# Two transformer layers on one core: weights of two key quarters added on GpSimd, and the query rests of a pair formed in one instruction

## The chip, the cores and the metric

The kernel runs on one core of one Trainium2 chip. The metric is the time of one execution on the device, in microseconds (us). The engines of the core are TensorE (PE in the profile, its weight loads PEld), VectorE (DVE), ScalarE (ACT), GpSimd (POOL) and SyncE (SP, whose queue issues DMAs). They run side by side and meet at semaphores.

## The reference, cut to what matters

Eight rows (sequences) of 512 tokens with 128 channels go through two layers. Each layer adds attention and a feed-forward part to its input. The change touches the attention of layer 1, with 16 query heads of 64 channels that share one set of keys and values:

```python
q = (x @ Wq + bq).reshape(B, S, H, DK)        # H = 16, DK = 64
k = x @ Wk + bk
v = x @ Wv + bv
scores = jnp.einsum('bshd,btd->bhst', q, k) / np.sqrt(DK)
w = jax.nn.softmax(scores, axis=-1)
out = jnp.einsum('bhst,btd->bshd', w, v).reshape(B, S, H * DV)
return out @ Wo + bo
```

The feed-forward part of layer 1 picks two of eight experts for each token. Layer 0 has an attention without softmax and a feed-forward part with weights and inputs rounded to four bits.

## The kernel before, in words

Every engine runs the same list of steps. A row of layer-1 attention is a round of 64 steps (k = 0 to 63), eight rounds in all (r = 0 to 7). A step handles one quarter of the keys (128) against all 512 queries of one head: `first` (L1446) computes the transposed scores in two matmuls (L1459, L1460), ScalarE exponentiates them into one of six buffers `wide` (L856). Two heads form a pair, eight steps of k: even steps one head, odd steps the other. Every fourth step, two steps later, `values` (L1470) takes four finished tiles: for each it runs two matmuls of 32 columns with the values (L1487), into bank `ps_out[0]`, and then one with a tile of ones (L1498), into `ps_out[1]`, which sums the weights over the keys, that is, gives the softmax's denominator. The four positions of 32 columns in the array hold the two heads and two key quarters side by side. The operands are float32, and each such matmul is two records in the profile. For the last two pairs of the last round (`direct`) the ones have their own form (L1495), left aside here.

At the end of a pair ScalarE copies both banks (L882, L887). SyncE stores the two partial sums per head, reloads them turned, VectorE adds and inverts them (L1227, L1228), and SyncE spreads the inverses (`sums_and_inverses`, L516). VectorE multiplies (L1241).

The scores use a split of the query into a rounded part and a rest. For each pair `query` makes 128 channels (two heads) in one bank of a ring of four (`ps_small`), ScalarE rounds it into `q_x` (L786), SyncE copies its halves four times into `q_hh` (L550), and VectorE's `lo_q` (L1031) writes the two rests straight into `q_lm`, one instruction per head (L1039). The maxima over keys come from matmuls (L1413) that go through the same ring, and VectorE reduces each (L1047).

In between lie the pieces of layer 0 for the next row (`l0`), placed at steps by `L0_AT` and, for VectorE, by `L0_DVE`, the gates and slots of the experts, and the projection (L1519). A layer norm needs an inverse root that GpSimd makes (`root`, L645). GpSimd further subtracts for the split of the expert weights in round 0 (L705), clears (L676) and scatters (L690) the experts' input rows, and scatters their results (L718). Its program before is a plain sequence: all that of one kind, then the next, each waiting for its data.

In round 7 the 23 expert tiles are inserted as steps of their own after k = 15, 23 and 31.

## Time and profile before

| | us |
|---|---|
| median of 3 runs | 1330.49 |
| lowest, highest | 1329.61, 1333.75 |
| the profiled execution, its own time | 1337.21 |
| its span in the trace | 1335.5 |
| mean granted clock of TensorE | 0.971 of full speed |

Busy time is the union of an engine's instructions; the chain is the work that ended last, followed back from the end. A matmul's end is modelled, so the pace of TensorE is read from the starts of neighbouring records. In the rows below a line number is that of the kernel before.

### The profile page before, as it was taken

What the parts mean: (1) busy time and instruction counts of PE and PEld (TensorE: products, weight loads), DVE (VectorE), ACT (ScalarE), POOL (GpSimd) and SP (SyncE); (2) the same over time, 40 slices, a digit from 0 to 9 for tenths busy, and PEclk for the clock granted to TensorE, in tenths of its full rate; (3) what the DMA queues carried; (4) which work ended last, traced back from release to release, by engine and by line L of the source; (5) the groups of instructions that cost most, each with busy time, mean ns of one, the idle gap of its engine ahead of it and who ended that gap; (6) DMA issues with size and microseconds to landing.
All of it is one profiled execution on the core that took longest, in us unless ns stands there. A gap on an engine that the chain in (4) does not pass through costs nothing.

```text
span 1335.5 us, 21832 instructions
## 1 busy us (share of the span) xinstructions
PE 1231.2 (92%) x7185; PEld 723.1 (54%) x7185; DVE 1008.1 (75%) x2396; ACT 682.9 (51%) x1252; POOL 262.2 (20%) x311
## 2 busy tenths in 40 slices
PE   5469999999999999999999999999999989999987
PEld 3235445554555455555554555455545468676743
DVE  6876888578867885788578857885787667677765
ACT  4036555544554456445544554455444466776631
POOL 2023223100210012001200120012000227263620
PEclk9559999999999999999999999999999989999988
DMA  2063574212321232224122412241221456474451
GB/s 79 0 174 100 187 211 153 62 50 58 115 64 49 58 113 58 58 57 113 49 62 54 120 42 61 63 119 36 61 67 46 155 164 233 139 241 159 132 199 48
DMA packets 89779, 133.80 MB, mean 100 GB/s; under 512 B 33292, under 2 KB 49228, under 8 KB 85700
## 3 DMA queue, kind: packets, MB, share of 16 engines
q1 hardware_dynamic: 75108, 99.80, 26.3%
q0 software_dynamic: 11344, 31.64, 7.2%
q8 instruction: 59, 0.97, 0.3%
q10 hardware_dynamic: 3216, 0.97, 0.3%
q14 instruction: 52, 0.43, 0.1%
HBM read 59.86 MB, written 38.68 MB: 74 GB/s over the span
## 4 chain that ended last, share of the span: by engine, by line
PE 63%; DVE 23%; issue 4%; ACT 3%; SPq 2%; DMA 2%; POOL 1%; another core or an unknown queue 0%; ACTq 0%; DVEq 0%; POOLq 0%
PE bank L1487 13%; PE bank L1459 6%; PE bank L1498 6%; PE bank L1413 5%; DVE mneg L1047 5%; PE bank L1460 5%; PE bank L1315 4%; PE bank L1317 4%; PE bank L1316 4%; DVE q_lm L1039 3%; PE bank L1519 3%; PE bank L1331 2%; PE bank L1321 2%; PE bank L1366 2%; PE bank L1356 1%
## 5 line engine op out<-in xcount | busy, mean ns | idle before, releaser
L856 ACT ACTIVATE wide<-bank 128x512 f32<-128x512 f32 x512 | 295.8, 600 | 324.1 <-PE bank L1460 314.2
L1047 DVE TENSOR_REDUCE mneg<-bank 128x1 f32<-128x512 f32 x512 | 329.4, 685 | 136.9 <-PE bank L1413 131.3
L1487 PE MATMUL bank<-wide,v_w 128*32 128x512 f32 x2048 | 248.0, 602 | 1.3 <-issue 1.0
L1459 PE MATMUL bank<-q_hh,k_hl 128*128 128x512 f32 x512 | 233.2, 456 | 14.3 <-ACT wide L856 11.1
L1460 PE MATMUL bank<-q_lm,k_h 65*128 65x512 f32 x512 | 203.6, 398 | 0.0
L1459 PEld LDWEIGHTS bank<-q_hh,k_hl 128*128 128x128 f32 x512 | 96.6, 189 | 135.6 <-issue 80.5
L649 POOL TENSOR_TENSOR rs<-rs,power 128x4 f32<-128x4 f32 x24 | 24.5, 1021 | 631.4 <-DVE rs L930 631.3
L1498 PE MATMUL bank<-wide,ones 128*32 128x512 f32 x992 | 129.2, 592 | 0.0
L718 POOL DMA_INDIRECT y_rows<-y_m,to_u x92 | 101.7, 1106 | 125.3 <-DVE y_m L1173 103.1
L1487 PEld LDWEIGHTS bank<-wide,v_w 128*32 128x32 f32 x2048 | 53.7, 109 | 122.7 <-issue 114.7
L1413 PE MATMUL bank<-k_a,q_x 128*128 128x512 f32 x256 | 107.5, 420 | 8.0 <-ACT hqt L776 2.6
L1039 DVE SCALAR_TENSOR_TENSOR q_lm<-bank,bq,q_x 64x512 fp32r<-64x512 f32 x128 | 95.6, 747 | 13.9 <-issue 11.5
L1413 PE MATMUL bank<-k_b,q_x 128*128 128x512 f32 x256 | 103.5, 404 | 2.3 <-DVE mneg L1047 2.1
L1460 PEld LDWEIGHTS bank<-q_lm,k_h 65*128 65x128 f32 x512 | 97.5, 190 | 11.6 <-issue 1.4
L690 POOL DMA_INDIRECT x_rows<-xr,slot_u x64 | 63.8, 997 | 170.3 <-DVE slot_u L1119 135.1
L882 ACT ACTIVATE raw<-bank 128x512 f32<-128x512 f32 x64 | 38.3, 598 | 107.9 <-PE bank L1498 93.4
L1281 DVE TENSOR_TENSOR part_l<-wide,part_h 128x512 fp32r<-128x512 f32 x92 | 62.0, 691 | 37.0 <-ACT wide L861 33.7
L861 ACT ACTIVATE part_h<-bank,b_t 128x512 fp32r<-128x512 f32 x92 | 63.5, 691 | 31.5 <-PE bank L1317 24.0
L1498 PEld LDWEIGHTS bank<-wide,ones 128*32 128x32 f32 x992 | 32.4, 111 | 74.9 <-issue 74.9
L1519 PE MATMUL bank<-wo,on 128*128 128x128 f32 x512 | 61.8, 280 | 4.8 <-DVE on L1241 4.8
L1413 PEld LDWEIGHTS bank<-k_a,q_x 128*128 128x128 f32 x256 | 49.1, 192 | 31.8 <-ACT q_x L786 13.5
L1519 PEld LDWEIGHTS bank<-wo,on 128*128 128x128 f32 x512 | 61.2, 196 | 7.4 <-DVE on L1241 6.2
(252 smaller groups left out, 1955.7 us busy)
## 6 DMA issues: line engine op xcount, KB each, us to landing
q_hh<-q_x SPq DMA_DIRECT2D x256, 128.0 KB
w_t<-w_rows SPq DMA_DIRECT2D x23, 1024.0 KB
x_rows<-part_h POOLq DMA_DIRECT2D x65, 258.0 KB, 5.0
inv<-inverse_scratch SPq DMA_DIRECT2D x124, 128.0 KB, 2.9
w_rows<-w_t SPq DMA_DIRECT2D x8, 1024.0 KB, 5.0
x_m<-x_rows SPq DMA_DIRECT2D x23, 258.0 KB
stage<-in_L_ffn_W SPq DMA_DIRECT2D x16, 256.0 KB, 4.7
yab<-y_rows POOLq DMA_DIRECT2D x8, 512.0 KB, 8.4
```

The source lines that it names most:

```text
L690: pool.indirect_dma_start(x_rows, bass.IndirectOffsetOnAxis(ap=slot_u[:, b, i:i + 1], axis=0), xr[:, i, :], None).then_inc(scattered, 16)
L718: pool.indirect_dma_start(y_rows, bass.IndirectOffsetOnAxis(ap=to_u[:, t % TO, i:i + 1], axis=0), y_m[:, t % YM, i, :], None).then_inc(y_s ...
L856: act.activation(wide[:, st.g % WIDE, :], ps, ACT.Exp, scale=SCALE1).then_inc(wide_full, 1)
L861: ins = act.activation(dst, ps, ACT.Gelu_apprx_tanh, bias=b_t[:, st.t % WT, st.m:st.m + 1])
L1039: ins = dve.scalar_tensor_tensor(q_lm[0:DK, gh % HEADS, :], ps[rows, :], bq[rows, h:h + 1], q_x[rows, pair % 2, :].bitcast(F32), ALU.add, ...
L1047: dve.tensor_reduce(mneg[:, pair % 2, col:col + 1], ps[:], X, ALU.max, negate=True).then_inc(free, 1)
L1413: into(("mx", 2 * pair + b, j), lambda ps: pe.matmul(ps[:], q_x[:, pair % 2, P * j:P * j + P], keys[:, n % 2, :], start=True, stop=True))
L1459: pe.matmul(ps, k_hl[:, n, t], q_hh[:, gh % HEADS, :], start=True, stop=False)
L1460: last = pe.matmul(ps, k_h1[0:DK + 1, n, t], q_lm[0:DK + 1, gh % HEADS, :], start=False, stop=True)
L1487: pe.matmul(ps_out[0][rows, :], v_w[:, n, c, TILE * d:TILE * d + TILE], weights, start=(c == 0), stop=(c == TT - 1))
L1498: last = pe.matmul(ps_out[1][rows, :], ones[:], weights, start=(half == 0), stop=(half == 1))
L1519: last = pe.matmul(ps[:, P * i:P * i + P], on[:, g % (H // 4), P * i:P * i + P], wo[:, g, :], start=(g == pairs.start), stop=(g == pairs.s ...
```

## The change

For each pair but the two direct ones, GpSimd adds the exponentiated tiles of two key quarters of the same head (steps k and k - 2, where k modulo 4 is 2 or 3), in two pieces of 256 columns, into `halves`. `values` no longer has the ones. `sums_of` runs four matmuls with ones once per pair, three steps after the pair's last, on the four added tiles; the two positions per head now hold the two half sums. ScalarE's copy of the sums comes one step later and waits for them (`summed`); ScalarE's reuse of a `wide` buffer waits for the addition too, and an addition waits for the previous pair's `summed`. VectorE's `lo_q` becomes one instruction for 128 channels into a single buffer `q_rest`, and SyncE copies its halves to `q_lm` (`copy_rests`); the semaphore for the copies of a pair counts to 96 instead of 64. GpSimd's program becomes one list over the steps, with roots, additions, splits, scatters and clearings at given steps. Besides, memory is laid over: `part_l` over weights of layer 0, `stage` over two of the four expert weight buffers, so that round 0 splits weights in two buffers instead of four.

```diff
-    L0_DVE = [-14, -11, -11, -10, -7, -6, -4, -2, 0, 0, 9, 10, 13, 17, 18, 21, 25, 26, 29, 30, 30, 31, 32,
-              34, 35, 37, 38, 39, 40, 42, 43, 44, 44]
+    L0_DVE = [-14, -13, -11, -10, -7, -6, -4, -2, 0, 0, 9, 10, 13, 17, 18, 21, 25, 26, 29, 30, 30, 32, 32,
+              34, 35, 37, 38, 39, 40, 42, 42, 44, 44]
...
+    ROOT_AT = [31, 43, 52]
+    SCATTER_AT = [[1, 4, 5, 8], [13, 16, 17, 20]]
+    LAST_SCATTER_AT = [[0, 0, 0, 0], [1, 1, 1, 1]]
+    ZERO_AT = [24, 25, 28, 29, 32, 33, 36, 37]
...
+    def adds(st):
+
+        return st.kind == "o" and st.k % TT >= 2 and added(pair_of(st))
...
-            names = [(("pv", pair), 0), (("ps", pair), 1)]
+            names = [(("pv", pair), 0)] + ([(("ps", pair), 1)] if direct(pair) else [])
+        elif st.kind == "o" and st.k % PAIR == PAIR - 1 and added(pair_of(st)):
+            names = [(("ps", pair_of(st)), 1)]
...
-        q_x = sb("q_x", [P, 2, S], F32R)
+        q_x, q_rest = sb("q_x", [P, 2, S], F32R), sb("q_rest", [P, S], F32R)
+        halves = sb("halves", [P, 2, 2, S])
...
+            def copy_rests(pair):
+
+                read_out(sp, ("q", pair))
+                for b in range(2):
+                    gh, here = 2 * pair + b, slice(DK * b, DK * b + DK)
+                    if gh >= HEADS:
+                        sp.wait_ge(first_full, last_step(gh - HEADS) + 1)
+                    sp.dma_start(q_lm[0:DK, gh % HEADS, :].bitcast(F32), q_rest[here, :].bitcast(F32)).then_inc(q_copied[pair % 2], 16)
...
+                if split_pair(st) is not None:
+                    copy_rests(split_pair(st))
...
+            def halve(st):
+
+                half, b, pair = st.k % PAIR // TT, st.k % 2, pair_of(st)
+                if pair:
+                    pool.wait_ge(summed, pair)
+                pool.wait_ge(wide_full, st.g + 1)
+                for q in range(2):
+                    cols = slice(S // 2 * q, S // 2 * q + S // 2)
+                    last = pool.tensor_tensor(halves[:, half, b, cols], wide[:, (st.g - 2) % WIDE, cols],
+                                              wide[:, st.g % WIDE, cols], ALU.add)
+                last.then_inc(halved, 1)
...
-            scatter(0)
-            for j in range(2 * E):
-                if SPLIT_STEPS[j] in (27, 45):
-                    root()
-                e, second = divmod(j, 2)
-                pool.wait_ge(expert_h, j + 1)
-                hi, lo = (w_t[:, e % WT, 2 * second + d, :] for d in range(2))
-                pool.tensor_tensor(lo, stage[:, j % 4, :], hi.bitcast(F32), ALU.subtract).then_inc(expert_l, 1)
-            for n in range(1, NB):
-                if n > 1:
-                    root()
-                    root()
-                if n + 1 < NB:
-                    root()
-                    zero(n + 1)
-                scatter(n)
-            for t in range(TILES):
-                read_out(pool, ("ty", t))
-                pool.wait_ge(to_set, t + 1)
-                for i in range(TT):
-                    pool.indirect_dma_start(y_rows, bass.IndirectOffsetOnAxis(ap=to_u[:, t % TO, i:i + 1], axis=0),
-                                            y_m[:, t % YM, i, :], None).then_inc(y_scattered[t % TO], 16)
+
+            for st in steps:
+                if st.kind == "o":
+                    if st.k in (ROOT_AT if st.r < NB - 2 else ROOT_AT[0:2] if st.r == NB - 2 else ()):
+                        root()
+                    if adds(st):
+                        halve(st)
+                    if st.r == 0 and st.k in SPLIT_STEPS:
+                        split_rest(SPLIT_STEPS.index(st.k))
+                    for b, at_ in enumerate(SCATTER_AT if st.r < NB - 1 else LAST_SCATTER_AT):
+                        for i in range(TT):
+                            if st.k == at_[i]:
+                                scatter(st.r, b, i)
+                    if st.k in ZERO_AT and st.r + 2 < NB:
+                        zero(st.r + 2, ZERO_AT.index(st.k))
+                if st.g is not None:
+                    here, i = divmod(st.g - 3, TT)
+                    if here - 2 in tile_of:
+                        scatter_y(tile_of[here - 2], i)
...
+                        if st.g - WIDE in add_of:
+                            act.wait_ge(halved, add_of[st.g - WIDE])
...
-                pair = pair_end(st, 1)
+                pair = pair_end(st, 2)
                 if pair is not None and not direct(pair):
-                    act.wait_ge(second_done, last_step(2 * pair + 1) + 1)
+                    act.wait_ge(summed, pair + 1)
...
-                for b in range(2):
-                    gh, rows = 2 * pair + b, slice(DK * b, DK * b + DK)
-                    h = gh % H
-                    if gh >= HEADS:
-                        dve.wait_ge(first_full, last_step(gh - HEADS) + 1)
-                    ins = dve.scalar_tensor_tensor(q_lm[0:DK, gh % HEADS, :], ps[rows, :], bq[rows, h:h + 1],
-                                                   q_x[rows, pair % 2, :].bitcast(F32), ALU.add, ALU.subtract)
-                ins.then_inc(free, 1)
+                if pair:
+                    dve.wait_ge(q_copied[(pair - 1) % 2], ((pair - 1) // 2 + 1) * 96)
+                p = pair % (H // 2)
+                dve.scalar_tensor_tensor(q_rest[:], ps[:], bq_two[:, p:p + 1], q_x[:, pair % 2, :].bitcast(F32),
+                                         ALU.add, ALU.subtract).then_inc(free, 1)
...
+            def sums_of(pair):
+
+                free_bank(("ps", pair))
+                pe.wait_ge(halved, add_of[last_step(2 * pair + 1)])
+                for half in range(2):
+                    for b in range(2):
+                        rows = slice(DK * b + TILE * half, DK * b + TILE * half + TILE)
+                        last = pe.matmul(ps_out[1][rows, :], ones[:], halves[:, half, b, :], start=True, stop=True)
+                last.then_inc(summed, 1)
...
-                            pe.matmul(ps_out[0][rows, :], v_w[:, n, c, TILE * d:TILE * d + TILE], weights,
-                                      start=(c == 0), stop=(c == TT - 1))
+                            last = pe.matmul(ps_out[0][rows, :], v_w[:, n, c, TILE * d:TILE * d + TILE], weights,
+                                             start=(c == 0), stop=(c == TT - 1))
+                        if added(pair):
+                            last.then_inc(second_done, 1)
+                if added(pair):
+                    return
                 for c in range(2 * half, 2 * half + 2):
                     for b in range(2):
                         weights = wide[:, (st.g - 3 + 2 * (c % 2) + b) % WIDE, :]
-                        if direct(pair):
-                            for d in range(2):
-                                rows = slice(DK * b + TILE * d, DK * b + TILE * d + TILE)
-                                last = pe.matmul(ps_out[1][rows, :], ones[:], weights, start=(c == 0), stop=(c == TT - 1))
-                        else:
-                            rows = slice(DK * b + TILE * (c % 2), DK * b + TILE * (c % 2) + TILE)
-                            last = pe.matmul(ps_out[1][rows, :], ones[:], weights, start=(half == 0), stop=(half == 1))
+                        for d in range(2):
+                            rows = slice(DK * b + TILE * d, DK * b + TILE * d + TILE)
+                            last = pe.matmul(ps_out[1][rows, :], ones[:], weights, start=(c == 0), stop=(c == TT - 1))
                         last.then_inc(second_done, 1)
...
+                pair = pair_end(st, 1)
+                if pair is not None and added(pair):
+                    sums_of(pair)
```

## Rows read from the trace of the kernel before

**Rows 1.** Page part 1: busy us, share of the span, instructions of each engine

```profile
PE 1231.2 (92%) x7185; PEld 723.1 (54%) x7185; DVE 1008.1 (75%) x2396; ACT 682.9 (51%) x1252; POOL 262.2 (20%) x311
```

**Rows 2.** Page part 4: the chain that ended last, by engine and by line

```profile
PE 63%; DVE 23%; issue 4%; ACT 3%; SPq 2%; DMA 2%; POOL 1%; another core or an unknown queue 0%; ACTq 0%; DVEq 0%; POOLq 0%
PE bank L1487 13%; PE bank L1459 6%; PE bank L1498 6%; PE bank L1413 5%; DVE mneg L1047 5%; PE bank L1460 5%; PE bank L1315 4%; PE bank L1317 4%; PE bank L1316 4%; DVE q_lm L1039 3%; PE bank L1519 3%; PE bank L1331 2%; PE bank L1321 2%; PE bank L1366 2%; PE bank L1356 1%
```

**Rows 3.** Windows: busy of PE, PEld, DVE, ACT, POOL, then clock, DMA

```profile
351.00:432.00 81.00, 79.48 (x483) 43.90 (x482) 58.48 (x130) 43.48 (x80) 8.04 (x9) 1.00 0.24 64
432.00:486.04 54.04, 51.51 (x323) 29.51 (x319) 45.96 (x129) 25.00 (x49) 7.62 (x12) 1.00 0.28 80
```

**Rows 4.** Chain by line of 351 to 432 us, then 432 to 486.04

```profile
by line: PE bank L1487 20.6%; PE bank L1459 10.3%; PE bank L1498 9.5%; PE bank L1413 8.1%; PE bank L1460 8.1%; PE bank L1519 4.4%; PE bank L1366 3.2%; issue 3.1%; PE bank L1356 3.0%; PE bank L1348 2.7%; PE bank L1331 2.4%; PE bank L1335 2.4
...
by line: DVE mneg L1047 15.1%; PE bank L1487 10.3%; DVE q_lm L1039 8.0%; PE bank L1498 5.6%; PE bank L1413 5.3%; PE bank L1459 4.2%; issue 4.0%; POOL rs L649 3.8%; PE bank L1460 3.5%; PE bank L1377 3.2%; PE bank L1315 2.4%; PE bank L1317 2.
```

**Rows 5.** Page part 5: name, count, busy us, mean ns, idle before

```profile
L1039 DVE SCALAR_TENSOR_TENSOR q_lm<-bank,bq,q_x 64x512 fp32r<-64x512 f32 x128 | 95.6, 747 | 13.9 <-issue 11.5
...
L1498 PE MATMUL bank<-wide,ones 128*32 128x512 f32 x992 | 129.2, 592 | 0.0
```

**Rows 6.** Timeline of PE: start us, us, engine, line, operation, count

```profile
566.40 1.04 PE L1498 MATMUL bank<-wide,ones 128*32 128x512 f32 x8
567.37 0.51 PE L1459 MATMUL bank<-q_hh,k_hl 128*128 128x512 f32 x1
567.71 0.40 PE L1460 MATMUL bank<-q_lm,k_h 65*128 65x512 f32 x1
567.95 0.40 PE L1413 MATMUL bank<-k_a,q_x 128*128 128x512 f32 x1
...
570.08 0.40 PE L1460 MATMUL bank<-q_lm,k_h 65*128 65x512 f32 x1
570.41 0.64 PE L1487 MATMUL bank<-wide,v_w 128*32 128x512 f32 x4
```

**Rows 7.** Groups by form on VectorE, one round, 351 to 486.04 us

```profile
L1056 DVE TENSOR_TENSOR x_l<-bank,x_h 128x512 fp32r<-128x512 f32 x1 | 0.7, 684 | 0.0
```

**Rows 8.** L662 and L705 on GpSimd: count, duration in ns min/median/max

```profile
L662 POOL TENSOR_TENSOR wk_l<-raw,wk_h x2: 311/325/339, 27.8 to 28.1; 128x64 fp32r<-128x64 f32 x2
...
L705 POOL TENSOR_TENSOR w_t<-stage,w_t x16: 1269/1282/1614, 119.2 to 205.7; 128x512 fp32r<-128x512 f32 x16
```

**Rows 9.** Four lines of VectorE: count, duration in ns min/median/max

```profile
L902 DVE TENSOR_SCALAR qs<-qs x43: 178/178/718, 9.1 to 981.2; 128x22 f32<-128x22 f32 x33, 128x32 f32<-128x32 f32 x8, 128x24 f32<-128x24 f32 x2
...
L910 DVE TENSOR_SCALAR t<-t x43: 343/344/1310, 10.4 to 985.2; 128x352 uint32<-128x352 uint32 x33, 128x512 uint32<-128x512 uint32 x8, 128x384 uint32<-128x384 uint32 x2
...
L934 DVE SCALAR_TENSOR_TENSOR rs<-rs x24: 161/163/1246, 6.9 to 1001.8; 128x4 f32<-128x4 f32 x24
...
L935 DVE TENSOR_TENSOR rs<-rs x24: 161/163/1207, 7.1 to 1002.0; 128x4 f32<-128x4 f32 x24
```

**Rows 10.** Timeline, subtractions of GpSimd beside one instruction of VectorE

```profile
163.00 2.51 POOL L705 TENSOR_TENSOR w_t<-stage,w_t 128x512 fp32r<-128x512 f32 x2
163.04 1.25 DVE L934 SCALAR_TENSOR_TENSOR rs<-rs 128x4 f32<-128x4 f32 x1
```

**Rows 11.** Timeline of SyncE's queue, four copies of queries

```profile
1047.25 3.19 SPq L550 DMA_DIRECT2D q_hh<-q_x  x4
```

**Rows 12.** Timeline of GpSimd, eight scatters before the last round

```profile
1037.13 1.04 POOL L690 DMA_INDIRECT x_rows<-xr,slot_u  x1 [35.27 <-DVE slot_u L1119]
...
1047.59 0.96 POOL L690 DMA_INDIRECT x_rows<-xr,slot_u  x1 [0.30 <-issue]
```

**Rows 13.** Timeline of ACT: exponentials of k 63 and 0, then of k 6

```profile
1038.57 1.09 ACT L856 ACTIVATE wide<-bank 128x512 f32<-128x512 f32 x2 [0.33 <-PE bank L1460]
...
1051.44 0.60 ACT L856 ACTIVATE wide<-bank 128x512 f32<-128x512 f32 x1 [2.74 <-PE bank L1460]
```

More of the change, by code:

```diff
@@ L188, in direct, with added, pair_of @@
         return pair >= (NB - 1) * (H // 2) + DIRECT
+    def added(pair):
+        return not direct(pair)
+    def pair_of(st):
+        return st.r * (H // 2) + st.k // PAIR
+    def adds(st):
+        return st.kind == "o" and st.k % TT >= 2 and added(pair_of(st))
     def tile_end(st):
@@ L408, in two_layers @@
         expert_h, expert_l = sem("expert_h"), sem("expert_l")
-        w_stored = [sem(f"w_stored{i}") for i in range(4)]
+        w_stored = [sem(f"w_stored{i}") for i in range(2)]
         small_full = [sem(f"small_full{i}") for i in range(SMALL)]
@@ new lines, in _ @@
+            for n in range(2):
+                for e in range(E):
+                    zero(n, e)
+            root()
+            for st in steps:
+                if st.kind == "o":
+                    if st.k in (ROOT_AT if st.r < NB - 2 else ROOT_AT[0:2] if st.r == NB - 2 else ()):
+                        root()
+                    if adds(st):
+                        halve(st)
[11 more added lines that the diff above has]
+                        scatter_y(tile_of[here - 2], i)
@@ L1474, in values @@
                 if half == 0:
-                    for name in (("pv", pair), ("ps", pair)):
-                        b, uses = out_place[name]
-                        if uses:
-                            pe.wait_ge(out_free[b], uses)
+                    free_bank(("pv", pair))
+                    if direct(pair):
+                        free_bank(("ps", pair))
                     if st.k == TT - 1:
```

87 lines of the change are left out of this document (54 added, 33 removed).

## Prediction

> **What bounds the kernel now.** I read the sums of the page first [rows 1]. TensorE shows 92% busy, VectorE 75%, GpSimd 20%, so TensorE is the first suspect and GpSimd has room. Busy is not the path, so the chain that ended last comes next [rows 2]: 63% of it is TensorE, 23% VectorE, 3% ScalarE, 1% GpSimd. The matmuls of the ones (L1498), which the change halves, are 6% of the chain, some 80 us of 1335.5, and the query rests (L1039), also halved, 3%, some 40 us. Then the windows: one round of attention, 351 to 486 us, has two parts [rows 3]. For 81 us TensorE is 79.5 us busy and VectorE only 58.5. For the last 54 us VectorE has 46.0 us of work (layer norms, gates, slots, next to the same maxima), and the chain there runs through VectorE's maxima at 15.1% and the rests at 8.0% [rows 4]. In the first part L1498 is 9.5% of the chain, in the second 5.6% [rows 4]: 7.7 and 3.0 us. So seven rounds are led first by TensorE and then by VectorE and TensorE in turn. The last round is filled up with the expert tiles, which the change leaves as they are.
>
> **Part 1, half of the tiles of ones go.** L1498 has 992 records [rows 5], 16 per pair, so 62 pairs. One block of eight starts at 566.40 and what follows it at 567.37: 0.97 us of TensorE, two blocks a pair [rows 6]. After the change each pair has one block: 62 x 0.97 = 60 us less. But the block no longer stands behind the products of values; it stands alone among score matmuls. Behind such an f32 block the next start-to-start step is 0.34 us (567.37 to 567.71) where the one after it is 0.24; ahead of one it is 0.33 (570.08 to 570.41) [rows 6]. So an isolated block costs another 0.10 + 0.09 us, about 0.19: 62 x 0.19 = 12 us back, and 48 us of TensorE's time stay. The chain has 10.7 us of L1498 in a round that spends 8 x 2 x 0.97 = 15.5 us on it, a share of 0.69 (over the kernel: 80 us of 120, 0.67). 48 x 0.67 = 32 us. Bounds: 12 us, if only the last part of the round counted and VectorE ate the rest, and 48. I take 32, as the two views agree.
>
> **Part 2, the query rests in one instruction.** Two instructions of 64x512 at 747 ns each [rows 5] become one of 128x512. The trace has no such form on 128 partitions; the nearest row, a VectorE subtraction of 128x512 with one operand in PSUM, takes 684 ns [rows 7]. The duration goes by columns, so the new one is put at 0.75 us, between 0.68 and 0.76. 64 pairs lose one of 747 ns: 48 us of VectorE. The chain has 40 us of the 95.6 [rows 2, 5], half goes: 20 us. Bounds: 10 us, if TensorE is late next in half of the places, and 25. The halves then travel by two more copies per pair on SyncE's queue. Four copies of the same kind take 3.19 us there [rows 11], 0.8 each, so 1.6 us per pair of 17 us (135 us by 8). They are wanted 13 steps later, at the pair's first scores, so I cost them at nothing; the cover is those 13 steps, and without it each pair would wait for a transfer of some us. The queue now waits at step 3 of eight for VectorE's rest, with the store of the sums behind it, and behind that the inverses. Those are used over ten steps later.
>
> **Part 3, the additions on GpSimd.** 62 pairs x 4 = 248 additions of 128x512 in two pieces each. GpSimd's nearest rows: 1282 ns for a two-input 128x512, 325 ns for 64 columns [rows 8]. A line through both gives 0.73 us for 256 columns; half of 1282 is 0.64. So an addition is 1.3 to 1.5 us, and a pair asks 5.1 to 5.8 us of GpSimd in 17. It has the room: it was busy 15.7 us in this round [rows 3]. A pair's last addition is ready some 2 us after its exponential, and TensorE asks for it three steps later, with a block of values in between. So in general it is hidden. ScalarE's reuse of a buffer of the ring of six asks for it four steps later.
>
> What isn't hidden is what it does to VectorE. In round 0 GpSimd already runs 16 such subtractions, and beside them VectorE's small instructions stretch: L902 718 ns against a median of 178, L910 1310 against 344, L934 1246 against 163, L935 1207 against 163 [rows 9]. L934 started at 163.04, just behind GpSimd's 163.00, and ended as the first of its two ended [rows 10]. The four are 0.54 + 0.97 + 1.08 + 1.04 = 3.63 us, by 16 additions 0.23 us each. 248 x 0.23 = 57 us more for VectorE, more than part 2 gives it. Of that about 0.3 lies on the path: VectorE is 23% of the whole chain [rows 2], and more where its small instructions are dense. 0.3 x 57 = 17 us. Bounds: 0, if the collisions fall in VectorE's idle time, and 57.
>
> The Trainium skill ("SBUF — State Buffer", section "Who interferes with whom") speaks against this change here: a VectorE instruction with two SBUF inputs, or in a 2-port mode, and a GpSimd instruction that reads SBUF exclude each other, and the second one waits for the whole of the first. The stretched rows agree, and by the rule a reader of PSUM such as the maxima stays free. By it two pieces give VectorE two waits of up to 0.64 us where one piece gave one of up to 1.28. A sum by the rule would put the same 57 us of delay at nearly the same size, so it stands.
>
> **Part 4, order on GpSimd.** The program's order is now one list by steps. A root (L649) can stand behind an addition, and VectorE's norm waits for it; GpSimd's roots are 3.8% of the chain in the second part [rows 4]. At three roots a round and 0.1 us more each: 2 us in all, between 0 and 8. In the last round eight scatters stand at steps 0 and 1, ahead of the additions of steps 2 and 3. They took 1037.13 to 1048.55, 11.4 us [rows 12]. Now they begin behind the addition of step 63, whose exponential ended at 1039.1 [rows 13], so at about 1041, and end at 1052.4. The addition of step 2 ends at 1053.8, and the exponential of step 6, at 1051.44 before [rows 13] and a us earlier now, waits for it: 3 to 4 us, once. I take 4, between 0 and 7.
>
> **Part 5, costed at nothing.** Buffers moved over one another, two weight buffers in round 0 instead of four (a store is asked for seven steps, some 15 us, ahead of its reuse), the few shifted steps of VectorE's list, and ScalarE's copy of the sums one step later.
>
> **The sum** is made against the profiled execution, 1337.21 us with a span of 1335.5: -32 - 20 + 17 + 2 + 4 = -29. The runs' median is 1330.49, 0.5% lower, and takes the same -29: 1301.5 us, a ratio of 0.978.
>
> **Rivals.** (a) The gain arrives nearly whole: collisions fall into VectorE's idle time, 22% of a round. For it: VectorE has 22 us idle in the first part [rows 3]. Against it: its dense work lies in the second part. -32 - 20 + 2 = -50, so 1280. (b) The path passes to the coupling of VectorE and TensorE and most of the gain is off the path: 12 of part 1, 10 of part 2, 17 and some 3 back, about -2 to -6, so 1326. For it: VectorE is 85% busy in the second part already; against it: the first part, 60% of the round, is TensorE's. (c) Slower: the two pieces of an addition each cost VectorE as much as one whole did, since tiny instructions in sequence are caught once per piece, as L934 and L935 were [rows 9]. Then an addition costs 0.46 us, 114 us in all, and two thirds of it reach the end, as maxima queue behind them and TensorE waits for their banks: +76 - 52 + 2 + 4 = +30, so 1360. It decides from 0.19 us per addition that reaches the end (46 of gain over 248). My forecast has 0.07. (d) The additions come late and TensorE waits for `halved` each pair, 0.5 us or more: -29 + 31 = +2, so 1333. For it: GpSimd is shared with roots that wait for VectorE; against it: the margin above.
>
> **How the numbers follow.** About 0.3%, 4 us, is what a measurement of this kernel can tell from no change. The forecast, with its own range of 1285 to 1318, has a chance of 0.58, (a) 0.18, (b) 0.10, (c) 0.09, (d) 0.05. Faster: 0.58 + 0.18 + 0.06 of (b) = 0.82. Same: 0.04 + 0.02 of (d) = 0.06. Slower: 0.09 + 0.03 = 0.12. The range reaches over (a) and (b), with the wider bounds of parts 1 to 3: 1273 to 1328.
>
> **What would show it.** The line of ones has half its records and its blocks stand alone; round time falls from 135 us to 131 or so, mostly in the first part. The rests show 64 instructions near 0.75 us. VectorE's two-input and SBUF-only instructions show raised means while the maxima stay at 685 ns. GpSimd's additions take 0.6 to 0.75 us a piece. TensorE's waits name GpSimd in no more than a few places, the last round's start among them. The prediction is wrong if VectorE's busy time rises by over 60 us with TensorE waiting for maxima, or if waits for GpSimd stand ahead of the ones in every pair.

## The result and the profile after

The changed kernel takes 1362.78 us, the median of four runs (1358.39 to 1369.60). The kernel before takes 1330.05 us beside it, in four runs (1328.62 to 1333.75). The ratio is 1.0245, with a 95% interval of 1.0209 to 1.0282: slower by some 33 us, where 29 us of gain were forecast. The time lies outside the range of 1273 to 1328. The profiled execution took 1363.96 us with a span of 1362.2.

The page of the changed kernel, part 1 and one line of part 2 (the granted TensorE clock in 40 slices, in tenths):

```profile
PE 1218.4 (89%) x6689; PEld 712.9 (52%) x6689; DVE 1022.2 (75%) x2332; ACT 681.9 (50%) x1252; POOL 638.0 (47%) x807
...
PEclk9569888999999999999998999999999989998988
```

Against [rows 1], TensorE ran 496 matmuls less and was busy only 12.8 us less, where 48 were forecast. VectorE lost 64 instructions of 747 ns, 48 us, and was busy 14.1 us more. The mean granted clock fell from 0.971 to 0.944.

Its groups, from part 5 of the page (busy us, mean ns of one | idle before, and what ended it):

```profile
L745 POOL TENSOR_TENSOR halves<-wide 128x256 f32<-128x256 f32 x496 | 379.6, 790 | 483.0 <-PE bank L1544 296.3
...
L1109 DVE TENSOR_REDUCE mneg<-bank 128x1 f32<-128x512 f32 x512 | 328.6, 683 | 130.5 <-PE bank L1475 127.0
...
L1544 PE MATMUL bank<-halves,ones 128*32 128x512 f32 x496 | 66.9, 612 | 0.3 <-POOL halves L745 0.2
```

The groups by form on VectorE, in the changed kernel:

```profile
L1303 DVE TENSOR_TENSOR on<-raw,inv 128x512 f32<-128x512 f32 x62 | 54.4, 877 | 10.9 <-DMA inv<-inverse_scratch 10.7
...
L1102 DVE SCALAR_TENSOR_TENSOR q_rest<-bank,bq_two,q_x 128x512 fp32r<-128x512 f32 x64 | 47.8, 747 | 9.2 <-issue 7.9 <-PE bank L1379 0.8
...
L1058 DVE TENSOR_TENSOR v<-v,lnw_row 128x512 f32<-128x512 f32 x8 | 9.2, 1149 | 0.0
```

and the first and the last of these in the kernel before:

```profile
L1241 DVE TENSOR_TENSOR on<-raw,inv 128x512 f32<-128x512 f32 x62 | 42.6, 686 | 8.8 <-DMA inv<-inverse_scratch 8.5
...
L993 DVE TENSOR_TENSOR v<-v,lnw_row 128x512 f32<-128x512 f32 x8 | 5.5, 686 | 0.0
```

The ones have half their records, and TensorE never stands ahead of them for GpSimd: 0.3 us of idle time in all. The rests are one instruction on 128 partitions, in the 747 ns that half of one took [rows 5]. The maxima, which read PSUM, keep their length (683 ns). What has grown most is VectorE's work with two operands in SBUF: the normalization of outputs takes 877 ns instead of 686, the layer norm's weights 1149 instead of 686. Some instructions with a single SBUF tensor have grown too. The one below took 348 ns before and 388 with the fills of experiment 2. Three such lines (L979, L1004, L1156) are 11 us longer in all than with the fills.

```profile
L979 DVE TENSOR_SCALAR t<-t 128x352 f32<-128x352 f32 x33 | 18.0, 545 | 0.2
```

One place in the middle of a round shows it (start, us, engine; in brackets the idle time before):

```profile
462.08 4.00 POOL L745 TENSOR_TENSOR halves<-wide 128x256 f32<-128x256 f32 x4 [1.10 <-ACT wide L921]
462.46 1.22 DVE L1058 TENSOR_TENSOR v<-v,lnw_row 128x512 f32<-128x512 f32 x1
...
463.71 1.11 DVE L1059 TENSOR_TENSOR v<-v,lnb_row 128x512 f32<-128x512 f32 x1
...
464.85 1.29 DVE L1109 TENSOR_REDUCE mneg<-bank 128x1 f32<-128x512 f32 x2
...
465.69 0.47 PE L1475 MATMUL bank<-k_a,q_x 128*128 128x512 f32 x1 [1.60 <-DVE mneg L1109]
```

Two layer-norm instructions are stretched beside four pieces of additions. The two maxima behind them start late, and TensorE stands still for 1.60 us until they have freed a bank. This is the step from a collision to the end of the kernel. The direct way, TensorE or ScalarE waiting for an addition, is nearly empty over the whole run. It is 0.2 us for TensorE, and this for ScalarE (who waits for whom: us in all, times, longest):

```profile
ACT wide L921 <- POOL halves L745: 2.1, 2, 1.4
```

**Where the time went.** I cut the span at the starts of ScalarE's copy of the bank of values, one per pair, 64 in all: to the first one, then eight pairs (round 0), 48 (rounds 1 to 6), and the end. The windows of after (us, busy of PE, PEld, DVE, ACT and POOL with instructions, granted clock, DMA share, GB/s):

```profile
0.00:119.91 119.91, 74.15 (x288) 47.02 (x289) 86.80 (x254) 43.24 (x85) 31.19 (x61) 0.77 0.35 90
119.91:271.76 151.85, 133.82 (x706) 71.95 (x707) 115.01 (x244) 76.26 (x144) 84.05 (x100) 0.91 0.51 151
271.76:1079.40 807.64, 756.11 (x4359) 417.39 (x4360) 631.15 (x1471) 396.54 (x755) 387.07 (x506) 0.98 0.33 85
1079.40:1362.20 282.80, 254.31 (x1339) 176.49 (x1339) 189.26 (x364) 165.82 (x269) 135.70 (x140) 0.94 0.53 169
```

and of the three attention windows of before, which no row ahead of the prediction cuts in this way:

```profile
123.72:258.95 135.23, 128.22 (x770) 69.58 (x770) 106.58 (x253) 75.30 (x144) 35.74 (x36) 1.00 0.51 154
258.95:1057.63 798.68, 773.28 (x4743) 431.01 (x4743) 619.14 (x1517) 398.66 (x755) 89.08 (x117) 1.00 0.26 71
1057.63:1335.50 277.87, 254.44 (x1371) 176.06 (x1370) 192.08 (x369) 165.66 (x269) 107.81 (x100) 0.96 0.51 166
```

The span grew by 26.7 us (the profiled execution of before was itself 6.7 us above its median): -3.8 ahead of the first mark, +16.6 in round 0, +9.0 in rounds 1 to 6, +4.9 at the end. Within a round (marks of a middle round; column i is the time from pair i's mark to the next, and so holds the steps of pair i + 1; worked out, not a view):

```
i                          0     1     2     3     4     5     6     7
before                  13.8  17.4  12.9  16.7  16.2  19.2  23.1  15.8
after                   12.7  16.9  12.3  18-20 16.8  20.3  21.9  16.3
change with fills       13.1  16.9  13.1  15.1  14.6  16.8  21.9  16.3
```

In columns 0, 1, 2 and 6 the change brings 0.5 to 1.2 us, where part 1 forecast 0.78 of TensorE per pair; in 7 it loses 0.5. In 3 to 5, where VectorE leads, it loses up to 3 us. The last line is an experiment below.

### The profile page after: what moved, and what is told of

The parts are those of the page before. It is cut to its first block and busy times, and to the rows that moved or that the text cites. A ratio compares the mean times of both kernels' runs of the same rounds, so it can differ in the third digit from the quotient of the medians.

```text
span 1362.2 us, 21768 instructions
## 1 busy us (share of the span) xinstructions
PE 1218.4 (89%) x6689; PEld 712.9 (52%) x6689; DVE 1022.2 (75%) x2332; ACT 681.9 (50%) x1252; POOL 638.0 (47%) x807
## 5 line engine op out<-in xcount | busy, mean ns | idle before, releaser
L745 POOL TENSOR_TENSOR halves<-wide 128x256 f32<-128x256 f32 x496 | 379.6, 790 | 483.0 <-PE bank L1544 296.3
L1563 PE MATMUL bank<-wide,v_w 128*32 128x512 f32 x2048 | 260.8, 629 | 1.0 <-issue 1.0
L1521 PE MATMUL bank<-q_hh,k_hl 128*128 128x512 f32 x512 | 237.9, 465 | 18.4 <-ACT wide L921 10.9
L1544 PE MATMUL bank<-halves,ones 128*32 128x512 f32 x496 | 66.9, 612 | 0.3 <-POOL halves L745 0.2
L1475 PEld LDWEIGHTS bank<-k_b,q_x 128*128 128x128 f32 x256 | 50.2, 196 | 25.7 <-DVE mneg L1109 14.2
L926 ACT ACTIVATE wide<-bank,b_t 128x512 f32<-128x512 f32 x92 | 62.9, 684 | 0.0
```

The lines of the kernel that those rows point to most:

```text
L745: last = pool.tensor_tensor(halves[:, half, b, cols], wide[:, (st.g - 2) % WIDE, cols], wide[:, st.g % WIDE, cols], ALU.add)
L926: ins = act.activation(dst, ps, ACT.Gelu_apprx_tanh, bias=b_t[:, st.t % WT, st.m:st.m + 1])
L1475: into(("mx", 2 * pair + b, j), lambda ps: pe.matmul(ps[:], q_x[:, pair % 2, P * j:P * j + P], keys[:, n % 2, :], start=True, stop=True))
L1521: pe.matmul(ps, k_hl[:, n, t], q_hh[:, gh % HEADS, :], start=True, stop=False)
L1544: last = pe.matmul(ps_out[1][rows, :], ones[:], halves[:, half, b, :], start=True, stop=True)
L1563: last = pe.matmul(ps_out[0][rows, :], v_w[:, n, c, TILE * d:TILE * d + TILE], weights, start=(c == 0), stop=(c == TT - 1))
```

## The experiments

Times compare with before on the same chip, as a ratio with its interval. Where I turn a ratio into microseconds, it is times 1330. Each theory's expectation was written before the run.

**1. Part 2 alone, and the change without part 2.**

```diff
 # e1: before, with this; likewise copy_rests on SyncE, counts 96
-                for b in range(2):
-                    ins = dve.scalar_tensor_tensor(q_lm[0:DK, gh % HEADS, :], ps[rows, :], bq[rows, h:h + 1], ...
+                dve.scalar_tensor_tensor(q_rest[:], ps[:], bq_two[:, p:p + 1], q_x[:, pair % 2, :].bitcast(F32),
+                                         ALU.add, ALU.subtract).then_inc(free, 1)
 # e2: the change, with the same lines the other way round
```

> The kernel before with only the rests of a pair formed in one instruction and copied by SyncE (and small buffers of the expert table laid over the comparisons, to make room). Theory (GpSimd's additions are what costs): this part is worth what it was put at, 10 to 25 us, so 1305 to 1320. Rival (the two more copies per pair hold SyncE's queue or come late): 1330 or more, with TensorE or SyncE waiting for copies of q_lm.

> The changed kernel with the rests formed as before, one instruction per head straight into q_lm. Theory: the rests bring 10 to 25 us in the changed kernel too, so this one takes 1373 to 1388. Rival (the rests by copy cost): 1350 or less.

The rests alone: 1326.48 us, ratio 0.9984 (0.9966 to 1.0001), so 2 us, hardly told from nothing. The change without them: 1382.04 us, ratio 1.0379 (1.0316 to 1.0443), so 50 us slower. So the additions and their list are the loss, and part 2 is worth 18 us on top of them (50 - 33, uncertain by some 10) but 2 by itself. VectorE's busy time fell as forecast, by 51 us (956.7 against 1008.1):

```profile
PE 1222.6 (93%) x7185; PEld 722.6 (55%) x7185; DVE 956.7 (72%) x2332; ACT 680.9 (52%) x1252; POOL 258.7 (20%) x311
```

Its profiled execution had a span of 1320.0, 15.5 less than before's. But that was the lowest of ten runs of this kernel, and before's profiled one was 6.7 us above its median. So I take the ratio, not the two spans.

**2. The same change without GpSimd's reads.** In this kernel GpSimd fills the buffer of halves with ones instead of adding weights; the sums over the keys are left out.

```diff
-                    last = pool.tensor_tensor(halves[:, half, b, cols], wide[:, (st.g - 2) % WIDE, cols],
-                                              wide[:, st.g % WIDE, cols], ALU.add)
+                    last = pool.memset(halves[:, half, b, S // 2 * q:S // 2 * q + S // 2], 1.0)
```

> The changed kernel with each addition replaced by two fills of the same pieces with ones: the sums over keys are wrong, all waits stay, GpSimd writes only and each piece takes some 0.3 us instead of 0.79. Theory (reads of GpSimd's additions hold up VectorE): VectorE's on (L1303) goes back from 877 to 685 ns, its busy time falls by about 60 us, the clock rises, and the time is 1285 to 1310. Rival (the order of GpSimd's list and its waits for summed cost): 1340 or more, and VectorE's durations matter little.

1306.88 us, ratio 0.9828 (0.979 to 0.9866): 23 us faster than before, 55 us faster than the change by the two ratios. Its page, its groups and rounds 1 to 6:

```profile
PE 1191.9 (92%) x6689; PEld 703.9 (54%) x6689; DVE 956.3 (74%) x2332; ACT 681.9 (53%) x1252; POOL 398.9 (31%) x807
```

```profile
L744 POOL MEMSET halves<- 128x256 f32 x496 | 141.9, 317 | 625.9 <-PE bank L1542 314.3 <-ACT wide L919 310.6 <-issue 0.9
...
L1301 DVE TENSOR_TENSOR on<-raw,inv 128x512 f32<-128x512 f32 x62 | 42.4, 684 | 10.7 <-DMA inv<-inverse_scratch 6.1 <-issue 4.4
```

```profile
259.90:1015.98 756.08, 737.52 (x4359) 414.27 (x4360) 580.30 (x1471) 396.96 (x755) 201.56 (x506) 1.00 0.34 91
```

Every instruction count is that of the change. VectorE is busy 956.3 us instead of 1022.2, and the normalization is back at 684 ns. TensorE, with the same 6689 matmuls, is busy 1191.9 instead of 1218.4: 26.5 us of its busy time in the change are the same work done more slowly, at a mean granted clock of 0.944 over the run where this kernel has 0.964. Of these, 18.6 us lie in rounds 1 to 6 (756.11 to 737.52) and 7.7 in round 0 (133.82 to 126.12). The profiled execution here was the lowest of its four runs (1299.45), which the comparisons of single executions below flatter by up to 7 us. But a fill differs from an addition in two ways, its reads and its length (317 against 790 ns). Experiments 5 and 6 take these up.

**3. The change's list without any additions.** All 62 pairs keep their 16 tiles of ones.

```diff
-        return not direct(pair)
+        return not direct(pair) and False
 # and in values(): the plain pairs' ones as before
```

> The changed kernel with no pair added: ones run as in the kernel before, GpSimd has no additions but works by the list over the steps, the rests are formed in one instruction, buffers are laid over as in the change. Theory: the list alone costs under 5 us against the rests alone, 1305 to 1325. Rival (the list's order, and two weight buffers in round 0, are the cause): over 1335, with round 0 longer than before by over 10 us.

1326.94 us, ratio 0.9962 (0.9943 to 0.9982). So halving the ones is worth 1.3% of ratio, 18 us (0.9962 to 0.9828), and the additions' reads and length cost 4.2%, 55 us (0.9828 to 1.0245). From the intervals, each of these two differences is uncertain by some 6 to 7 us. The windows of this kernel, round 0 and rounds 1 to 6:

```profile
120.82:265.05 144.23, 132.37 (x770) 71.31 (x770) 99.31 (x245) 75.20 (x144) 40.84 (x45) 0.96 0.56 168
265.05:1044.67 779.62, 767.29 (x4743) 431.48 (x4743) 579.38 (x1469) 396.83 (x755) 86.34 (x113) 1.00 0.34 87
```

In rounds 1 to 6 TensorE's busy time falls from 767.29 here to 737.52 with the ones halved: 29.8 us for 48 pairs, 0.62 each, where 0.97 - 0.19 = 0.78 was forecast. And round 0 takes 144.2 us, against 135.2 before and 136.8 with the rests alone: the list itself costs there.

**4. One piece instead of two.**

```diff
-                for q in range(2):
-                    cols = slice(S // 2 * q, S // 2 * q + S // 2)
-                    last = pool.tensor_tensor(halves[:, half, b, cols], wide[:, (st.g - 2) % WIDE, cols], ...
+                last = pool.tensor_tensor(halves[:, half, b, :], wide[:, (st.g - 2) % WIDE, :],
+                                          wide[:, st.g % WIDE, :], ALU.add)
```

> The changed kernel with each addition as one instruction of 512 columns instead of two of 256. Theory (what counts is how long GpSimd reads): VectorE's delay per addition stays, 1355 to 1372. Rival (c) of the prediction (each piece catches an instruction of its own): half of the delay goes, some 30 us, so 1340 or less.

1377.62 us, ratio 1.0367 (1.0321 to 1.0412): 16 us slower than the change. Its groups:

```profile
L743 POOL TENSOR_TENSOR halves<-wide 128x512 f32<-128x512 f32 x248 | 325.6, 1318 | 543.9 <-PE bank L1542 323.4 <-ACT wide L919 218.4 <-issue 0.3
...
L1301 DVE TENSOR_TENSOR on<-raw,inv 128x512 f32<-128x512 f32 x62 | 62.3, 1006 | 10.6 <-DMA inv<-inverse_scratch 10.5
```

One piece holds GpSimd for less in all (325.6 against 379.6 us), yet VectorE is busy 1036.8 us instead of 1022.2. So two pieces are the better form, and rival (c), by which it was the pieces that double the cost, is wrong in its mechanism.

**5. A GpSimd instruction that reads one operand.** The copy takes the place of the addition, so one key quarter of each two is left out of the sums.

```diff
-                    last = pool.tensor_tensor(halves[:, half, b, cols], wide[:, (st.g - 2) % WIDE, cols],
-                                              wide[:, st.g % WIDE, cols], ALU.add)
+                    last = pool.tensor_copy(halves[:, half, b, cols], wide[:, st.g % WIDE, cols])
```

> The changed kernel with each addition replaced by a copy of one of its two operands, in the same two pieces: the sums miss half of the keys, all waits stay, GpSimd reads one operand instead of two. Theory (GpSimd's reads hold VectorE for as long as they last): pieces of 0.3 to 0.4 us, VectorE's on (L1303) at 700 to 780 ns, and a time between that of the fills (1307) and of the change (1363): 1310 to 1335. Rival (only two-operand additions do it): 1307 or less and on at 685 ns.

1307.14 us, ratio 0.9843 (0.981 to 0.9875), not to be told from the fills.

```profile
L745 POOL COPY halves<-wide 128x256 f32<-128x256 f32 x496 | 202.6, 438 | 573.1 <-PE bank L1543 294.3 <-ACT wide L920 278.3
...
L1302 DVE TENSOR_TENSOR on<-raw,inv 128x512 f32<-128x512 f32 x62 | 44.0, 709 | 10.1 <-DMA inv<-inverse_scratch 9.9
```

VectorE is busy 962.3 us, 6 more than with fills, where the additions make it 66 more. By length alone 438/790 of 66 would be 37 us. Yet a copy does hold VectorE. In each kernel some normalizations start together with a piece on GpSimd (start, us; with additions of 256 columns, of 512, with copies, with fills; x2 is two pieces):

```profile
449.13 1.27 DVE L1303 TENSOR_TENSOR on<-raw,inv 128x512 f32<-128x512 f32 x1
449.13 1.86 POOL L745 TENSOR_TENSOR halves<-wide 128x256 f32<-128x256 f32 x2
...
868.69 1.82 DVE L1301 TENSOR_TENSOR on<-raw,inv 128x512 f32<-128x512 f32 x1
868.69 1.27 POOL L743 TENSOR_TENSOR halves<-wide 128x512 f32<-128x512 f32 x1
...
816.83 0.94 DVE L1302 TENSOR_TENSOR on<-raw,inv 128x512 f32<-128x512 f32 x1
816.84 1.20 POOL L745 COPY halves<-wide 128x256 f32<-128x256 f32 x2
...
938.68 0.68 DVE L1301 TENSOR_TENSOR on<-raw,inv 128x512 f32<-128x512 f32 x1
938.68 0.55 POOL L744 MEMSET halves<- 128x256 f32 x2
```

By itself the normalization takes 0.68 us. Beside an addition whose first piece took 0.72 it takes 0.59 longer, beside one of 1.27 it takes 1.14 longer, beside a copy of 0.39 it takes 0.26 longer, and beside a fill of 0.30 no longer. So where both start together, VectorE is held for the length of GpSimd's instruction less 0.13 us, whether that reads one operand or two, and this instruction isn't held at all where GpSimd only writes. What parts copies from additions is first of all their length: a meeting costs 0.26 us instead of 0.59. If meetings also become fewer by the same factor, 66 us shrink to 13 (an estimate from these numbers). Why only 6 arrive, that is, which instructions the shorter pieces happen to meet, was not followed up.

The Trainium skill ("SBUF — State Buffer", section "Who interferes with whom") says that a VectorE instruction with two SBUF inputs contends with a GpSimd instruction that reads SBUF. The trace agrees: additions (686 to 877 ns on average) and copies (709 ns on average, 0.94 us at the meeting above) hold such an instruction, fills don't (684), and the maxima, which read PSUM, don't move beside additions (683).

**6. VectorE's delay without any collision.** Is it VectorE's lost time that reaches the end, or something else that additions do? This kernel is the one with fills, and VectorE runs 33 small extra instructions in each of rounds 1 to 6, in steps 34 to 57, where the collisions were densest.

```diff
+                    if 0 < st.r < NB - 1:
+                        for _ in range(extra.get(st.k, 0)):
+                            link(dve.tensor_tensor(pad[:], pad[:], pad[:], ALU.add))
 # pad is 128x48; extra gives 1 or 2 in 22 of the steps 34 to 57
```

> The run with fills in place of additions (1307 us, sums wrong), plus 33 small VectorE instructions of some 0.22 us on a scratch tile in steps 34 to 57 of rounds 1 to 6, that is the 7 us a round by which VectorE's busy time grew there through the additions, with nothing on GpSimd. Theory (the whole loss is VectorE's time in the part where TensorE waits for its maxima, and the clock that falls with each wait): rounds 1 to 6 grow from 127.7 us to 133 to 138, as in the change (136.5), with a clock under 1.00 in pairs there, and the whole to 1335 to 1365. Rival (GpSimd's late additions hold up TensorE or ScalarE, beyond VectorE's time): rounds stay under 131 us and the whole under 1325.

1341.38 us beside 1340.07 for before, ratio 1.0018 (0.9991 to 1.0045): 25 us more than the fills alone (0.9828). The added group and rounds 1 to 6:

```profile
L1339 DVE TENSOR_TENSOR pad<-pad 128x48 f32<-128x48 f32 x198 | 40.4, 204 | 4.5
```

```profile
260.70:1052.33 791.63, 747.57 (x4359) 415.29 (x4360) 617.67 (x1669) 397.63 (x755) 199.02 (x506) 0.99 0.33 87
```

Over rounds 1 to 6, against the fills' window: VectorE busy +37.4 us, the stretch +35.6. The change against the fills: VectorE busy +50.9, the stretch +51.6. In both, by profiled executions, a microsecond of VectorE in these places is about a microsecond of the kernel; by whole times it is less here, 25 of 40. The two executions come from two chips, on which before took 1331.17 and 1340.07, so the ratio is the safer of the two. So a delay of VectorE alone, with no collision behind it, makes the kernel slower by two thirds of its length or more.

It brings the slower TensorE with it too. Over rounds 1 to 6 TensorE's busy time rose by 10.1 us over the fills' (747.57 to 737.52), where the additions made it 18.6 (756.11). In column 3 the granted clock of this kernel was 0.91 in four of six rounds; in the change it was 0.91, 1.00, 0.91, 0.85, 1.00 and 0.92 there. In column 5 this kernel stayed at 18.9 us and 1.00, where the change mostly had 20.3 at 0.92. One window of each kernel, column 3 of round 1, the change first:

```profile
313.68:333.50 19.82, 16.66 (x89) 8.52 (x90) 17.43 (x36) 7.21 (x17) 9.61 (x13) 0.91 0.34 96
...
303.87:322.31 18.44, 16.64 (x89) 8.47 (x90) 16.21 (x42) 7.19 (x17) 3.26 (x10) 0.91 0.31 85
```

The delay put in was smaller (40 to 66 us), it was in rounds 1 to 6 only, and it fell on fixed steps where collisions fall anywhere. Which of these leaves the other 8.5 us of busy time in rounds 1 to 6 was not tried and stays open.

**7. Additions only where TensorE leads.** From the table of pairs (pair 0's steps lie in column 7, pair 1's in column 0, and so on): additions in pairs 0, 1, 2 and 7 of rounds 1 to 6, 24 pairs in all. Ahead of it, to have four weight buffers in round 0 as before, stage is laid over the halves.

```diff
 # e7: experiment 3, with this, and w_t[:, e % WT, ...] and four w_stored for e % 2 and two
+        halves = nc.alloc_sbuf_tensor_at("halves", [P, 2, 2, S], F32, offset=half_at)
+        stage = nc.alloc_sbuf_tensor_at("stage", [P, 4, S], F32, offset=half_at)
 # e8: e7 with
-        return not direct(pair) and False
+        return not direct(pair) and 0 < pair // (H // 2) < NB - 1 and pair % (H // 2) in (0, 1, 2, 7)
```

> The list by steps and the rests in one instruction, no additions, and round 0 splits the expert weights in four buffers as before (the stage laid over the place of halves, which isn't used). Theory (the 7 us that round 0 lost in the run of the list without additions come from the two buffers: ScalarE waits for a store before it can split): round 0 takes 137 us or less, against 144.3, and the whole 1315 to 1323. Rival (the order of GpSimd's list did it): round 0 stays over 142 us and the whole at 1327.

> As the run with four buffers, plus the additions and single blocks of ones for pairs 0, 1, 2 and 7 of rounds 1 to 6, the places where TensorE leads and VectorE has few instructions that share the port: 24 pairs of 62. Theory (an addition costs nothing where VectorE has slack): about 2 us a round less than without additions, 1303 to 1313. Rival (the reads cost wherever they are): as without additions or above, 1320 or more.

e7, no additions: 1325.13 us, ratio 0.996 (0.9938 to 0.9983), as without the four buffers. e8: 1312.91 us, ratio 0.9869 (0.985 to 0.9888), 17 us faster than before and 50 faster than the change.

```profile
L748 POOL TENSOR_TENSOR halves<-wide 128x256 f32<-128x256 f32 x192 | 141.8, 764 | 277.2 <-ACT wide L924 196.4 <-PE bank L1551 80.8
```

```profile
267.38:1036.54 769.16, 752.75 (x4567) 424.30 (x4568) 596.22 (x1471) 397.17 (x755) 229.07 (x306) 1.00 0.35 90
```

By ratios, 24 pairs bring 12 us (0.996 to 0.9869), 0.5 each; rounds 1 to 6 of the profiles shrink by 10.3 (779.5 to 769.2). Their 96 additions still make VectorE busy 16.6 us more (969.9 against 953.3), 0.17 each, and yet most of TensorE's 0.62 per pair arrives: there VectorE's idle time pays for most of it.

**8. Round 0's order on GpSimd.** Two mends of e8: the first moves roots and clearings to later steps of round 0, the second puts GpSimd's work of round 0 in before's order.

```diff
 # e11: e8 with
+                    if st.k in ([27, 45, 52] if st.r == 0 else ROOT_AT ...
+                    clear_at = ZERO_AT if st.r else [52, 53, 54, 55, 56, 57, 58, 59]
 # e13: e8 with round 0 written out ahead of the loop over steps: scatter(0) whole,
 # the splits with roots ahead of the two at 27 and 45, the last root, zero(2) whole
```

> As the run with the additions where TensorE leads, but in round 0 GpSimd's roots stand at steps 27 and 45, ahead of the splits of those steps as in the kernel before, and the clearing of row 2's zones comes after the splits, at steps 52 to 59. Theory (round 0's 10 us come from roots queued behind splits that wait for ScalarE, and from clearings that share the DMA engines with the staging): round 0 falls from 146 to 138 us or less and the whole to 1302 to 1308. Rival (they come from something else in round 0, such as the scatters' places): round 0 stays over 143 us, 1313.

> As the run with the additions where TensorE leads, but GpSimd goes through round 0 in the order of the kernel before (scatters, then all splits with two roots between, a root, the clearing) and takes up the list by steps from round 1 on. Theory (round 0's 10 us come from the list's order there): round 0 at 138 us or less, as in the run of the rests alone, and the whole at 1302 to 1308. Rival (something else that the change did to round 0): 143 us or more, 1313.

e11: 1314.32 us, ratio 0.9861 (0.9832 to 0.9889). e13: 1318.92 us beside 1340.07, ratio 0.9842 (0.9824 to 0.986). The intervals of e8, e11 and e13 overlap. Round 0 by the profiles: 144.2 (experiment 3), 147.5 (e7), 146.0 (e8), 142.6 (e11), 139.6 (e13), against 136.8 with the rests alone. The four weight buffers changed nothing for the better (144.2 to 147.5), so it isn't they. In e7 two waits of the stretch 152 to 175 us name the cause in part (who waits for whom: us in all, times, longest):

```profile
POOL w_t L738 <- ACT w_t L891: 16.7, 3, 7.7
...
DVE rs L1006 <- POOL rs L695: 5.3, 1, 5.3
```

GpSimd's list stands at a split that waits for ScalarE, and a root that VectorE's norm needs stands behind it. The order accounts for some 6 of the 8 to 10 us of round 0 (146.0 to 139.6), by one profile of each. The whole times don't bear it out beyond 0.3%, within their intervals, and the three spans are 1311.0, 1312.6 and 1312.3.

## Why the prediction was wrong, step by step

**What bounds the kernel.** Right: the first part of a round is TensorE's, the second VectorE's. The table of pairs and e8 both bear it out.

**Part 1, -32 (12 to 48).** Measured -18 by ratios (experiments 3 to 2), uncertain by some 6. TensorE's share was 0.62 us per pair instead of 0.78. The sign and the bounds hold, the term is too large by some 14 us. In rounds 1 to 6 of the two profiled executions 23.5 us arrived (779.62 to 756.08), where the forecast's 32 for 62 pairs gives 25 for these 48. So the share of the chain isn't shown to be at fault, and where the rest went stays open.

**Part 2, -20 (10 to 25).** The instruction's 0.75 us is exact (747 ns). Its worth is 2 us alone and 18 on top of the additions. The forecast took it as one number for both. The first is below its lower bound; that TensorE's work was late next there is the reason I would give, and is only argued.

**Part 3, the additions' collisions: +17 (0 to 57).** This is the step that failed. The VectorE time was well sized: 66 us (1022.2 - 956.3), 0.27 per addition, where 57 and 0.23 were forecast from [rows 9]. Some luck is in it: the four rows counted are not where most of the 66 us arose (the normalizations and layer norms aren't among them). What failed is "of that about 0.3 lies on the path". 55 us of the 66 reached the end, a share of 0.83. The 0.3 was made of VectorE's share of the whole chain [rows 2], which is an average over stages. The collisions need work of VectorE on SBUF, mostly with two operands, and that is dense in the second part of a round (layer norms, gates, normalizations), where VectorE is 85% busy [rows 3] and the maxima queue behind it. There a delay of VectorE's own is a delay of the kernel, by 25 of 40 us in whole times and 35.6 of 37.4 in one pair of executions (experiment 6). And there was more than VectorE's wait: with the same matmuls TensorE was busy 26.5 us longer than with fills, which no term held. In rounds 1 to 6 it was 18.6 us longer beside +50.9 of VectorE, and in experiment 6, without collisions, 10.1 beside +37.4, so delays of VectorE alone bring a large part of it. Two windows of the change, column 5 of two rounds, show its size at one place, and a third the worst place of round 0:

```profile
350.28:370.55 20.27, 18.68 (x119) 11.41 (x118) 17.60 (x57) 6.82 (x16) 6.71 (x9) 0.92 0.19 41
761.73:780.41 18.68, 17.10 (x119) 11.06 (x118) 16.21 (x50) 6.82 (x15) 6.71 (x9) 1.00 0.21 46
...
166.71:191.91 25.20, 19.60 (x89) 9.76 (x90) 21.07 (x37) 8.98 (x20) 13.97 (x17) 0.80 0.52 160
```

The same 119 matmuls took 1.58 us more at a granted clock of 0.92 than at 1.00: part of that stretch ran at the lower level, 1.2 GHz. With the clock left aside, 18.68 is still 1.9 us above the 16.8 of the fills, the plain delay.

**Part 4, +6.** Its terms were not where the loss lay. VectorE's waits for GpSimd's roots are 16.4 us in all, against 19.2 before. The list cost most in round 0, by its order there (experiment 8). The scatters before the last round aren't the loss either: ScalarE waited 0.72 us for the addition behind them, where 3 to 4 were forecast. At the end of the run there was a wait that I had not looked for. GpSimd's loads of expert rows (yab) are issued behind the last additions, at 1308.01 instead of 1278.74. Counted from the start of the last stretch (1079.40 and 1057.63) that is 7.5 us later:

```profile
1306.75 1.92 PE L1563 MATMUL bank<-wide,v_w 128*32 128x512 f32 x16
...
1308.01 6.11 POOL L786 DMA_DIRECT2D yab<-y_rows  x8
...
1312.52 1.14 DVE L1261 SCALAR_TENSOR_TENSOR xres<-yab,gate,xres 128x128 f32<-128x128 f32 x4 [7.58 <-DMA yab<-y_rows]
...
1319.98 0.38 PE L1480 MATMUL bank<-ident,mneg 128*8 128x128 f32 x1 [7.08 <-DVE mneg L1109]
...
1320.29 3.64 PE L1563 MATMUL bank<-wide,v_w 128*32 128x512 f32 x16
```

VectorE waits 7.58 us for them, TensorE 7.08 for VectorE, and the block of 16 matmuls behind it takes 3.64 us, where the one at 1306.75 takes 1.92: the lower level of the clock. Before had such a block there as well, of 3.64 us at 1288.47. The pair took 27.5 us against 16.4 before, the one ahead of it 12.85 against 19.37: 4.6 us in sum. But this doesn't mark the additions. With fills the loads are as late (228.6 us behind that start in both), and the last stretch takes 281.7 us. With the additions of experiment 4 it takes 277.4, no more than before's 277.9. So the wait is real, and its price in the whole isn't shown.

**Part 5, at nothing.** Right for the two weight buffers (e7). Wrong for the list: round 0's 144.2 us against 136.8. In rounds 1 to 6 it cost nothing (779.6 against 783.1).

**The rivals.** (a) needed collisions in idle time: e8 shows that this nearly holds for its 24 pairs, where TensorE leads, and the change shows that it doesn't for all. (c) named the right time (1360 against 1362.8), and the right second half, maxima queueing and TensorE waiting for banks with most of it reaching the end. Its first half, the doubling by pieces, is wrong (experiment 4). It set 0.19 us per addition reaching the end as the point from which it decides; 55/248 = 0.22 arrived. (d) is wrong: TensorE waited 0.2 us in all for GpSimd ahead of the ones. The sum by ratios is now -18 for the ones, -2 for the rests alone, -3 for list and buffers (0.9984 to 0.9962), +55 for the additions: +32, against the 33 measured.

## What to carry to other kernels

Price an engine's lost time by the slack of the place where it is lost, and never by that engine's share of the whole chain: some 0.2 us of VectorE per addition took little from the gain in the stretches where TensorE leads (0.5 of 0.62 us per pair arrived), and a delay of VectorE in the other stretches cost two thirds of itself or more. When idle GpSimd takes work off a busy TensorE, first list the VectorE instructions on SBUF, above all those with two operands, that will run beside it, and give it only the stretches where VectorE has room: with 24 of the 62 pairs the kernel was 17 us faster than before (12 of them from the additions), with all 62 it was 33 us slower. And when an engine gets more work in its stream, look at every DMA that it issues behind it.

## What the runs showed of the hardware

- Beside GpSimd additions of two SBUF operands, a 128x512 VectorE operation with two SBUF operands went from 686 to 877 ns on average (pieces of 256 columns, 790 ns each) and to 1006 ns (one piece of 512, 1318 ns). Beside copies of one operand (438 ns) it took 709, beside fills (317 ns) 684.
- Where such an operation and GpSimd's instruction started together, it took longer by GpSimd's length less 0.13 us: 0.59 us beside an addition of 0.72, 1.14 beside one of 1.27, 0.26 beside a copy of 0.39, nothing beside a fill of 0.30.
- VectorE operations with one SBUF tensor can be held as well: a TENSOR_SCALAR of 128x352 went from 348 ns before to 545 beside the additions, with 388 beside fills.
- A VectorE scalar_tensor_tensor from PSUM of 512 columns takes 747 ns on 128 partitions as on 64.
- Where TensorE waited for VectorE's maxima, the windows of a pair had a granted clock of 0.80 to 0.92, that is partly 1.2 GHz, in some rounds and 1.00 in others: the pair with the wait of 1.60 us above (451.12 to 469.11) stayed at 1.00. With the same 6689 matmuls TensorE's busy time was 1191.9 us with fills and 1218.4 with additions.
